# A gated cross-attention and expert kernel: the opening and the tail of its first passage in a new order, each expert's weights split one step later

## The reference, cut to what matters

```python
x = x + tanh(g_xattn[0]) * L0_xattn(layernorm(x), ctx, ctx, mask)   # softmax over 77 keys per batch
x = x + tanh(g_ffn[0])   * L0_ffn(layernorm(x), ...)                # 8 experts, the best 2 per row, and a shared expert
x = x + tanh(g_xattn[1]) * L1_xattn(layernorm(x), ctx, ctx, ...)    # softmax over the rows (axis 1)
x = x + tanh(g_ffn[1])   * L1_ffn(layernorm(x), ...)                # integer weights times 1/127

# L0_ffn
gate_dense = top2(softmax(xt @ gate_w.T + gate_b))
expert_e   = (silu(xt @ w1[e].T + b1[e]) * (xt @ w3[e].T + b3[e])) @ w2[e].T + b2[e]
z          = (silu(xt @ ws1.T + bs1) * (xt @ ws3.T + bs3)) @ ws2.T + bs2
y          = sum over e of gate_dense[:, e] * expert_e
return y + z
```

## Time and profile before

| | us |
|---|---|
| median of three runs | 639.9 |
| lowest and highest of them | 637.91, 640.18 |
| the profiled execution, its own time | 644.34 |
| its span, first to last instruction | 641.4 |
| mean granted TensorE clock | 0.986 |

### The profile page before, as it was taken

The page is one execution under the profiler, slowest core; times in us unless marked ns, Lnnn a source line. Parts: engine busy times, 40 slices in busy tenths (PEclk is TensorE's granted clock), DMA queues, the critical chain, the costliest instruction groups (busy, mean ns, idle before and its releaser), DMA issues.

```text
span 641.4 us, 12684 instructions
## 1 busy us (share of the span) xinstructions
PE 604.0 (94%) x3562; PEld 496.6 (77%) x3562; DVE 444.2 (69%) x1321; ACT 363.7 (57%) x806; POOL 249.9 (39%) x315
## 2 busy tenths in 40 slices
PE   7899999889998999999999999998889999999997
PEld 6667887767776888888888878776757767867886
DVE  4888887866765666666666654777667787757655
ACT  6587778846643555555555543444555664664633
POOL 4445564535461254223223237766253543101100
PEclk9899899979999999999999999999899999999999
DMA  7445664444187833333333217631111511100000
GB/s 204 143 137 177 213 222 156 167 168 147 61 300 222 274 100 107 106 102 108 100 109 102 96 63 270 251 95 53 30 50 58 162 45 56 44 1 33 34 34 33
DMA packets 46656, 77.51 MB, mean 121 GB/s; under 512 B 7604, under 2 KB 31615, under 8 KB 46335
## 3 DMA queue, kind: packets, MB, share of 16 engines
q1 hardware_dynamic: 38521, 57.55, 27.3%
q0 software_dynamic: 7344, 19.14, 9.0%
q10 hardware_dynamic: 726, 0.02, 0.1%
HBM read 44.52 MB, written 32.17 MB: 120 GB/s over the span
## 4 chain that ended last, share of the span: by engine, by line
PE 53%; DVE 17%; issue 9%; ACT 8%; POOL 7%; DMA 4%; SPq 1%; ACTq 0%; POOLq 0%; DVEq 0%
PE bank L1162 11%; PE bank L1164 10%; PE bank L1163 10%; PE bank L1601 5%; POOL yr L624 4%; PE bank L1622 3%; PE bank L1623 3%; PE bank L1463 3%; PE bank L1454 2%; DVE xa L2076 2%; DMA rows_by_expert<-n,pos 2%; PE bank L1561 2%; DVE sl L2154 2%; DVE st L2085 1%; ACT sl L1008 1%
## 5 line engine op out<-in xcount | busy, mean ns | idle before, releaser
L582 POOL TENSOR_TENSOR yg<-yg,b 128x256 f32<-128x256 f32 x71 | 52.2, 735 | 116.4 <-ACT yg L699 116.4
L2037 DVE TENSOR_TENSOR hb<-bank,b 128x512 f32<-128x512 f32 x71 | 49.1, 692 | 60.2 <-PE bank L1164 59.9
L536 POOL DMA_INDIRECT rows_by_expert<-n,pos x64 | 65.8, 1027 | 57.8 <-DVE pos L1889 41.3
L1601 PE MATMUL bank<-n4Th,wint 128*128 128x512 f32 x192 | 74.5, 408 | 5.2 <-DVE sl L2154 3.8
L624 POOL DMA_INDIRECT yr<-expert_out,out_row x64 | 66.8, 1043 | 20.4 <-issue 17.0
L699 ACT ACTIVATE hTh<-bank 128x256 fp32r<-128x256 f32 x71 | 27.4, 386 | 83.0 <-PE bank L1463 83.0
L1601 PE MATMUL bank<-n4Tl,wint 128*128 128x512 f32 x192 | 71.9, 395 | 0.0
L699 ACT ACTIVATE g3h<-sl 128x512 fp32r<-128x512 f32 x60 | 37.8, 631 | 44.4 <-DVE sl L2154 34.3
L1164 PE MATMUL bank<-w13h,xTl 128*128 x142 | 56.6, 399 | 0.0
L1163 PE MATMUL bank<-w13l,xTh 128*128 x142 | 56.3, 396 | 0.0
L1162 PE MATMUL bank<-w13h,xTh 128*128 x142 | 55.9, 394 | 0.2 <-DVE xTl L2044 0.2
(11 more groups left out here) (299 smaller groups left out, 1782.1 us busy)
## 6 DMA issues: line engine op xcount, KB each, us to landing
xg<-rows_by_expert SPq DMA_DIRECT2D x71, 128.0 KB, 2.1
expert_out<-yg SPq DMA_DIRECT2D x71, 128.0 KB, 1.7
stage<-in_wexp SPq DMA_DIRECT2D x24, 256.0 KB, 3.8
x_shared<-x SPq DMA_DIRECT2D x8, 512.0 KB, 2.8
xa<-x_shared SPq DMA_DIRECT2D x4, 1024.0 KB, 7.3
out<-ost SPq DMA_DIRECT2D x8, 512.0 KB, 2.6
xin<-in_x SPq DMA_DIRECT2D x7, 512.0 KB, 4.8
wint<-in_wint POOLq DMA_DIRECT2D x3, 768.0 KB, 11.0
```

What stands on the lines that cost most here:

```text
L536: pool.indirect_dma_start(out=xs, out_offset=bass.IndirectOffsetOnAxis(ap=pos[p][:, k, j:j + 1], axis=0), in_=n2[p][:, j, :], in_offset=No ...
L582: pool.tensor_tensor(yg[s], yg[s], b2[:, bass.ds(e, 1), :].rearrange("p a d -> p (a d)"), ALU.add)\
L1601: last = mm(bank[:, 2 * (m % 2) + w, :], wt[:, k, m * P:(m + 1) * P], part[c][:, k, :], start=(q == 0 and k == 0), stop=(q == 1 and k == K ...
L2037: tt(hb[p], bank[:, p, :], b13[:, bass.ds(e, 1), :].rearrange("p a n -> p (a n)"), ALU.add)\
```

## The change

It moves work and adds none, apart from the count of products that nobody reads.

- SP: the two gains are loaded behind the first three weight chunks, then `load_x(1, 1)`, the first context rows, four further small inputs, and the rest of the context. ScalarE issues no DMA. In a step the order is `store_late`, `load_x`, `store_mid`, `load_expert`.
- Experts: step g splits expert g - 1 on ScalarE and VectorE; expert 7 is split in the tail. The wait on `setup_copied` and `l1_out` goes from step 6 to step 7. The buffers of the split bias and of the router's weights move to the place of expert 6's low part. The wait for the low parts moves from ahead of the load of `b13` to ahead of that of `b2`.
- POOL subtracts no weights any more; VectorE does all six chunks, two of them in step 1.
- Opening: new orders on ScalarE, VectorE and TensorE. `shared_bias` and `ln1_stats(2, 0, 1)` go from the opening to step 1 on VectorE, behind `route_b`. On POOL `rstd_first(2)` stays ahead of the loop.
- Step 1 on TensorE: `probs_t`, `t2_half(1)`, `up(f, 1)`, `values`, `up(f, 2)`, `gate`.
- Third passage, VectorE: a new order of the operations around `residual3(0)`, and `x2(3, (1,))` one operation later.

The diff, cut to its core:

```diff
 # SP
+            small(gains_raw[:, 0:2], i["g_xattn"].partition_broadcast(P), "gains_in")
+            small(gains_raw[:, 2:4], i["g_ffn"].partition_broadcast(P), "gains_in")
+            load_x(1, 1)
             small(ctxr[0:64, 0, :], ctx_rows[0:64, 0, :], "ctxr_in")
             small(ctxr[64:KV, 0, :], ctx_rows[64:KV, 0, :], "ctxr_in")
-            load_x(1, 1)
+            small(gwf.rearrange("p k e -> p (k e)"), i["gate_w"])
+            small(bs2f, i["bs2"].partition_broadcast(3))
+            small(bs13.rearrange("p a m -> p (a m)"), i["bs13"])
+            small(gbias, i["gate_b"].partition_broadcast(P))
...
-                load_expert(g)
                 if load:
                     load_x(g + 2, p)
-                if store:
-                    store_mid(g - 1, 1 - p)
+                store_mid(g - 1, 1 - p)
+                load_expert(g)
 # POOL
             rstd_first(0)
-            shared_low(0, 1)
-            shared_low(1, 1)
+            rstd_first(1)
             rstd_half(0)
-            rstd_first(1)
-            shared_low(4, 2)
             rstd_half(1)
-            shared_low(5, 2)
             pool.memset(zeros, 0.0).then_inc(sem("filled"), 1)
             pool.memset(ones8, 1.0).then_inc(sem("filled"), 1)
             rstd_first(2)
 # ScalarE, step
                 if ffn:
                     silu(f, 0)
-                if g > 1:
-                    pt_copy(g)
+                pt_copy(g)
+                if g == 1:
+                    t2_copy_half(1)
...
-                if g > 1:
-                    expert_high(g, 0)
+                expert_high(g - 1, 0)
...
-                expert_high(g, 1)
+                expert_high(g - 1, 1)
...
-                expert_high(g, 2)
+                expert_high(g - 1, 2)
 # ScalarE, opening
-            for c in range(2):
-                stage_high(c, wsh[:, c, :], 1)
+            stage_high(0, wsh[:, 0, :], 1)
             act.wait_ge(sem("mask_ready"), 1)
             scores_copy_half(0)
             scores_copy_half(1)
+            stage_high(1, wsh[:, 1, :], 1)
+            softmax_half(0)
+            act.wait_ge(sem("gains_in"), 32)
+            act.activation(gains, gains_raw, ACT.Tanh).then_inc(sem("gains_done"), 1)
+            pt_copy_half(0)
+            softmax_half(1)
             stage_high(2, wsh[:, 2, :], 1)
-            act.wait_ge(sem("small_in"), 16 * 6)
-            act.activation(gains, gains_raw, ACT.Tanh).then_inc(sem("gains_done"), 1)
-            softmax_half(0)
-            softmax_half(1)
-            pt_copy_half(0)
             t1_copy(1, (0, 3))
             pt_copy_half(1)
-            for c in range(3):
+            stage_high(0, wsh[:, 3, :], 2)
+            scores_copy(1)
+            ln2_apply(0, 0, range(2))
+            softmax(1, (0, 2))
+            t2_copy_half(0)
+            softmax(1, (2, 4))
+            for c in (1, 2):
                 stage_high(c, wsh[:, 3 + c, :], 2)
-            ln2_apply(0, 0, range(2))
-            scores_copy(1)
-            t2_copy_half(0)
-            softmax(1)
             ln2_apply(0, 0, range(2, GT))
-            pt_copy(1)
-            t2_copy_half(1)
 # TensorE, opening
             probs_t_half(0)
-            keep_warm(2)
             t1_second()
             values_half(0)
             probs_t_half(1)
+            scores(1, 0)
             values_half(1)
-            keep_warm(1)
-            scores(1, 0)
+            scores_back(1)
...
+            keep_warm(6)
             t2_half(0)
-            scores_back(1)
-            keep_warm(2)
+            keep_warm(4)
 # VectorE, step
                 if g == 1:
-                    for c in range(3):
-                        expert_low(0, c)
-                else:
-                    expert_low(g, 0)
+                    shared_bias()
+                    ln1_stats(2, 0, 1)
+                expert_low(g - 1, 0)
...
-                if g == 1:
-                    expert_low(1, 0)
-                expert_low(g, 1)
-                expert_low(g, 2)
+                expert_low(g - 1, 1)
+                expert_low(g - 1, 2)
 # VectorE, end of the opening
-            residual_half(0)
-            ln2_stats_half(0)
-            ln1_stats(1, 1, 0)
-            prob_scale_half(1)
+            row_max(1)
             residual_half(1)
+            t2_low_half(0)
             low_part(0, wsh[:, 3, :], wsl[:, 3, :], 2)
             ln2_stats_half(1)
-            t2_low_half(0)
-            row_max(1)
...
-            shared_bias()
-            t2_low_half(1)
-            ln1_stats(2, 0, 1)
 # VectorE, third passage
             late_hidden(2, 2)
-            late_low(2, 2)
+            residual3(0)
             late_hidden(2, 3)
-            shift3(0, 2)
-            late_low(2, 3)
-            residual3(0)
             stats4(0)
             x3_read(0)
+            late_low(2, 2)
+            late_low(2, 3)
+            shift3(1, 0)
             residual3(1)
-            shift3(1, 0)
             stats4(1)
             x3_read(1)
             late_out(2, 0)
+            shift3(0, 2)
             n4_low(0)
+            shift3(1, 1)
             late_out(2, 1)
-            shift3(1, 1)
```

More of the change, by code:

```diff
@@ L160, in flamingo_kernel @@
         w0.put("raw_pad", [P, GT * D * 7], F32)
-        bs2f = w0.put("bs2f", [3, D], F32)
-        part = [w0.put(f"bs2_part{c}", [3, D], BF16) for c in range(3)]
-        pick = w0.put("bs2_pick", [3, D], F32)
-        gwf = w0.put("gwf", [P, KD, NE], F32)
         maski = w0.put("maski", [KV, B], I32)
@@ L206, in flamingo_kernel @@
         vo0 = ck3.put("vo0", [P, B, D], F32)
+        ck4 = Area(area_a + (2 * NE - 2) * w13_size, area_a + (2 * NE - 1) * w13_size)
+        bs2f = ck4.put("bs2f", [3, D], F32)
+        part = [ck4.put(f"bs2_part{c}", [3, D], BF16) for c in range(3)]
+        pick = ck4.put("bs2_pick", [3, D], F32)
+        gwf = ck4.put("gwf", [P, KD, NE], F32)
         shift_sum = [cb.put(f"shift_sum{p}", [P, NG * 2 * GT], F32) for p in range(2)]
@@ L352, in _, with step @@
                 sp.dma_start(stage[c], i["wsh"][(c + 3) * P:(c + 4) * P, :]).then_inc(sem(f"stage_in{c}"), 16)
-            def step(g, p, load=True, store=True):
-                if store and g - 1 < HALVED:
+            def step(g, p, load=True):
+                if g - 1 < HALVED:
                     store_late(g - 1)
-                load_expert(g)
                 if load:
                     load_x(g + 2, p)
-                if store:
-                    store_mid(g - 1, 1 - p)
+                store_mid(g - 1, 1 - p)
+                load_expert(g)
             load_x(2, 0)
@@ L417, in _ @@
                 load_tile(t, t)
+            for c in range(3):
+                sp.wait_ge(sem(f"low_done{c}"), NG + 2)
             small(b2, i["b2"].partition_broadcast(P), "b2_in")
@@ L747, in softmax @@
                 act.wait_ge(sem("pscale_done"), 2 * halves(g - 1))
-                for j in range(GT):
+                for j in range(*tiles):
                     act.activation(probs[:, j, :], bank[:, 6, j * P:j * P + KV], ACT.Exp, bias=negmax[:, j:j + 1],
@@ L1282, in step @@
                     up(f, 1)
+                values(g, b)
                 if g == 1:
-                    probs_t(1)
-                    t2_half(1)
-                values(g, b)
-                if ffn:
-                    if g == 1:
-                        pe.wait_ge(sem("bias_ready"), 1)
+                    up(f, 2)
+                    pe.wait_ge(sem("bias_ready"), 1)
+                    gate(f)
+                    gate_back(f)
+                elif ffn:
                     gate(f)
@@ L1406, in _ @@
             last.then_inc(sem("ctx_mean"), 1)
+            keep_warm(6)
             t2_half(0)
-            scores_back(1)
-            keep_warm(2)
-            for c in range(3):
-                pe.wait_ge(sem(f"low_done{c}"), 1 if c else 2)
+            keep_warm(4)
+            pe.wait_ge(sem("low_done0"), 1)
+            pe.wait_ge(sem("low_done1"), 1)
             for g in range(1, NG):
@@ L1898, in step @@
                     hidden(f, 0)
+                if g == 1:
+                    t2_low_half(1)
+                    low_part(1, wsh[:, 4, :], wsl[:, 4, :], 2)
+                    low_part(2, wsh[:, 5, :], wsl[:, 5, :], 2)
                 residual1(g, p, g // 2)
@@ L1957, in _ @@
             dve.wait_ge(sem("pool_const"), 17)
+            low_part(0, wsh[:, 0, :], wsl[:, 0, :], 1)
             row_max_half(0)
             row_max_half(1)
-            low_part(2, wsh[:, 2, :], wsl[:, 2, :], 1)
+            low_part(1, wsh[:, 1, :], wsl[:, 1, :], 1)
             dve.wait_ge(sem("gains_done"), 1)
             prob_scale_half(0)
-            chained(cp(gwh, gwf))
-            tt(gwl, gwf, gwh, ALU.subtract).then_inc(sem("bias_ready"), 1)
-            chained(ts(fgain, gains[:, 3:4], DEQ * DEQ, None, ALU.mult))
-            dve.memset(rank_base, 0.0).then_inc(sem("base_done"), 1)
+            ln1_stats(1, 1, 0)
```

(7 more changed lines are left out.)

39 lines of the change are left out of this document (19 added, 20 removed).

## The result

| | before | after |
|---|---|---|
| median, us | 640.0 | 649.6 |
| lowest and highest | 637.91, 640.29 | 649.56, 650.37 |
| the profiled execution, its own time | 644.34 | 649.57 |
| its span | 641.4 | 647.5 |
| mean granted TensorE clock | 0.986 | 0.987 |

The change makes the kernel slower: the ratio is 1.0147 (95% interval 1.0119 to 1.0176), 9.4 us, where 0.7 us was forecast. The two medians are 9.6 us apart, but the two profiled executions only 6.1, since the one of before was 4.3 above its own median. That difference is part of what follows.

A forecast was written before the change was run, and what follows sets the result against it. TensorE was nearly always busy, with a ring over the engines setting common steps; -4.5 + 0.5 + 9.5 + 0 - 4.3 = +1.2, less 0.5 absorbed, gave +0.7: 640.6 us on the 639.9 median, range 635.5 to 645.5.

The forecast's parts named there:

- The stall on POOL: Step 1: rstd_first(2) waits for statistics ahead of rstd_second(1); with the opening, step 2 starts 9.5 us later, ends +7 and +12.
- hold-up of some 0.7 us: Step 1: subtractions moved to VectorE can hold up POOL's root once; the sum would be +1.4 instead of +0.7.
- Step 6: Shared-expert loop: ScalarE's 5.12 us wait for a weight chunk goes, saving 4.5 us of a 4.98 excess; ends -5.0 and -3.0.
- the 0.5 kept back: Step 6: 0.5 us withheld from the gain because the stores still go out, beside the scatter the ring waits for.
- The scatters: Common loop steps: late rows go out some 3 us later, nearer the last scatters; +0.5 us over four steps.
- rival 3: Loop steps: late rows and stores of keys and values lie in front of the scatters; slower, 645.1 us, chance 0.18.
- the sign of being wrong: No idle time in step 1, or common steps longer than 20.3 us with a scatter landing after more than 5 us.
- The last passage: Before the last passage: VectorE's new order lets t4(1) start at 452.1 instead of 456.46, -4.3 us; ends -4.6 and -1.5.
- The clock loss that the ring was to absorb: Steps 2 to 5: TensorE's part of the clock loss is partly absorbed by its waits of 1.09 and 1.90; -0.5 us.
- the ring: Shared-expert loop: scatter, norm, operand split, sum and statistics, next scatter, across engines; said to set 19.5 us a common step.
- The opening and the tail: First product near 22.7 (21.85 before), likely at full clock; route_b ends at 38.0; tail costs 0, up to +1 us.

The follow-up runs named there:

- e3: Kernel before with only shared_bias and ln1_stats(2, 0, 1) moved from VectorE's opening to step 1, behind route_b; ratio 1.0167, +9.7 us against before.
- e12: Kernel before with only the experts' split one step later, SP's loads and stores ordered as in the change; ratio 1.0040, 2.4 us slower than before.
- e4: Kernel before with only VectorE's new order ahead of the last passage; ratio 0.9977, 2.9 us below before.
- e14: Kernel of e13 with VectorE's new order ahead of the last passage; ratio 0.9964, 2.7 us below before.
- e13: Kernel of e12 with store_late(g) ahead of load_expert(g) on SP; ratio 0.9992, 0.2 us below before.
- e15: The kernel of e8 unchanged, run again beside e14 on one chip; ratio 0.9965, 2.9 us below before.
- e2: Changed kernel with POOL's rstd_first(2) and the memset of vo0 behind rstd_second(1) instead of ahead of the loop; 644.0 us, 3.0 above before.
- e1: Kernel before, unchanged, profiled once more; 640.5 us, 0.5 below before.
- e6: Kernel of e5 with ln1_stats(2, 0, 1) back in VectorE's opening, shared_bias staying in step 1; 2.6 us above before.
- e5: Kernel of e2 with store_late(g) ahead of load_expert(g) on SP; 642.15 us, 1.4 above before.
- e9: Kernel of e4 with the stores of the kept keys and values moved to step 5, behind the input load; ratio 0.9972, 3.0 us below before.
- e10: Kernel of e8 with the stores of the kept keys and values moved to step 5, behind the input load; ratio 0.9930, 4.7 us below before.
- e8: Kernel of e5 with shared_bias back in VectorE's opening, ln1_stats(2, 0, 1) staying in step 1; ratio 0.9895, 6.1 us below before.
- e11: Changed kernel, unchanged, run again on the slower chip; 666.3 us, ratio 1.0111 against before there.

## Why the prediction was wrong

The measured parts add up to the result: e3 +9.7, e12 +2.4, the last passage -2.9 (e4) or -2.5 (e14 less e13), together 9.2 to 9.6 against 9.6. Each has an interval of some 2 us, so the exactness is luck: by the ratios, which use every run, in place of the medians the same parts make 11.5 to 11.8 against 9.4. The new opening by itself has nothing left to explain (e15 less e14: -0.2).

- **The stall on POOL: right, with a second one overlooked.** Forecast +9.5, measured +9.7 in e3 and 10.4 at the start of step 2 in the pair of profiles. Place and chain came as said: POOL's terms for group 1 done at 46.5 (46.8), an idle of 5.42 us ahead of the next products (5 to 7), low clock, `up(1, 0)` at 56.67 (54 to 58). POOL's first operation for group 2 took 0.92 us at 42.03, beside a subtraction of VectorE, and 0.23 before: the hold-up of some 0.7 us that the prediction had named as possible and left out of the sum. But there is a second part, the bias product's wait of 2.03 for `shared_bias`. The forecast looked at the statistics behind `shared_bias` and never asked who else waits for `shared_bias` itself. That wait, and not POOL's, is where the clock fell. So the 9.5 met a cost of two stalls with a price worked out for one; POOL's order alone gives back 5.7 to 6.6 (e2), which makes the closeness of the number partly luck.
- **Step 6, -4.5: the step that failed.** The wait does go, as forecast: with before's order ScalarE waits 3.6 to 5.4 us at the chunk in step 6 (four profiles), with the later split 0.8 at most (eleven). What failed is the price. The 4.98 us excess over step 5 was read from one execution in which the clock had fallen, and was then taken off the median. Over all profiles step 6 takes 21.00 to 24.44 with before's order (mean 22.6) and 20.30 to 21.76 with the later split (mean 21.1), so 1.5 us less on average, and the time shows nothing of it: e13 is at -0.2, with an interval of -2.1 to +1.1. Where the clock holds in both, step 6 takes 20.92 us in e13 and 21.00 in e1. That the execution lay 4.3 above its median isn't due to step 6 either: against e1 its seventh pass starts 0.3 later. The wait was also put down to the chunk alone, though `l1_out` stands one line ahead of it in the code; the stores don't go away with the change, they lie beside the last scatter of step 6, and the 0.5 kept back for that was not tested apart.
- **The scatters, +0.5 (ends -1.5 and +4): mis-sized.** It is +2.6 (e12 less e13). The mechanism was seen (late rows nearer the scatters) and named as rival 3, at 4.0, and the sign of being wrong that the prediction gave came true: steps 4 and 5 take 20.88 and 21.33 us in after, and ScalarE goes on 5.4 and 5.8 us after the last scatter was issued (4.2 at the earlier trace rows). No row of before priced it. Together with step 6 this part was forecast at -4.0 and measured at +2.4, 6.4 us of the 8.9 missed.
- **The last passage, -4.3: right in kind, too large.** 2.5 to 2.9, as the old order takes 17.7 to 18.4 us from out3(0) to t4(1) in the other executions and took 19.0 in the one that was read, and as the new one takes 15.33 where the forecast's replay makes 14.6 (452.1 less 437.46). That makes 1.4 to 1.8 us of the miss.
- **The clock loss that the ring was to absorb, -0.5: not seen.** e3's whole cost is 9.7 where 9.5 less 0.5 was the sum.
- **The opening and the tail.** `up(0, 0)` came at 22.43 (22.7) and at full clock, as forecast (1.00 from 22 to 26 us, where before has 0.66 and 0.50), `route_b` ended at 37.2 (38.0), and the tail cost nothing that stands out: from `up(7, 0)` to out3(0) it is 262.4 us before and 262.5 after.

The sum was right about the large loss and wrong about all that was to pay for it, each time towards the gain.

## What to carry to other kernels

An excess that one profile shows belongs to that execution: before a gain is taken off the median, see in a second profile whether the stretch is as long there, whether the clock fell in it, and whether what comes behind it starts any later for it. A wait that is taken out of a loop's head is paid wherever its DMAs go next, so look for the transfer that the ring itself waits for and keep the queue's bulk stores away from it. And of an operation moved behind others, list all who wait for it, not only the one that waits longest.

## What the runs showed of the hardware

- TensorE's clock can make a wait dearer than its length. Behind an idle of 2.21 us it stayed at 1.00 (e1), behind 2.78 and 3.33 it fell to 0.50 and 0.54 (e6, e4), and one us more of waiting went with 2.7 us more of step. But the length of the one idle time doesn't decide: at the same product, the first with the shared bias, it fell to 0.50 behind 2.03 us in after and stayed at 1.00 behind 2.04 in e5; behind 2.06 it was 0.50 from 41 to 44 us in e2. In step 7 of e9 it fell behind 1.22 (0.57 from 158 to 162 us), and in e10 it stayed at 1.00 behind 1.24 at the same place.
- The last indirect scatter from POOL lands about 1 us later where 512 KB or more of stores go out among a step's scatters: ScalarE goes on 5.4 and 5.8 us after its issue in steps 4 and 5 of after, 4.3 and 4.4 in e5, and 5.4 and 6.1 in step 6 of e13 and e14, beside the kept stores. The DMA share doesn't tell the cases apart: it is 1.05 in after from 124 to 128 us, but 0.98 in e5 from 112 to 116 as well, and in step 5 of e15, without such stores, ScalarE goes on only after 5.9 us, though the share had fallen to 0.13 two us before.
- The same kernel took 17 us longer on one chip (that of e8 to e11), nearly all of it between step 7 and the third passage: from step 7 to out3(0) the changed kernel takes 303.1 us in e11 and 287.8 in its first profile. The signs against before were the same there; e8's gain was 6.1 us on it and 2.9 on the other.
